# Decoder layer on one core: transposes in halves of 64 rows with new engine orders, cross attention's output weights folded into k^T v, and the local output projection as three products

## The reference

```python
def attn(x):     # 16 heads of 64, causal; rows are keys, columns queries of the score matrix as written
    q, k, v = einsum('ahe,bce->bach', W, x)          # for W_Q, W_K, W_V
    p = softmax(where(tril, einsum('bach,baCh->bacC', k, q), -1e10) / 8)
    return einsum('aeh,bach->bce', W_O, einsum('bacC,baCh->bach', p, v))

def xattn(x, ctx):  # linear attention, 16 heads of 16
    q, k = 1 + elu(x @ Wq.T + bq), 1 + elu(ctx @ Wk.T + bk);  v = ctx @ Wv.T + bv
    k = where(mask, 0, k);  q = l2norm over tokens(q);  k = l2norm over head features(k)
    kv = einsum('bhnd,bhne->bhde', k, v)
    return einsum('bhnd,bhde->bhne', q, kv) @ Wo.T + bo

def layer(x):    # twice: local attention, windows of 128, 8 heads of 64, then an MLP
    q, k, v = split(shift_token(x) @ wqkv)
    q, k = rotary_xpos(l2norm(q) * qs, l2norm(k) * ks)
    x = x + softmax(8 * q k^T over own and previous window) v @ wo
    a, g = split(layernorm(shift_token(x)) @ w1 + b1)
    return x + (a * gelu(g)) @ w2 + b2

x = x + attn(layernorm(x));  x = x + xattn(layernorm(x), ctx);  x = x + (layer(layer(z)) of z = layernorm(x))
```

## Time and profile before

| | us |
|---|---|
| median of 3 runs | 1154.78 |
| lowest, highest | 1153.16, 1154.82 |
| profiled execution | 1154.38 |
| its span, first to last instruction | 1152.6 |

### The profile page before, as it was taken

The page is one execution under the profiler, slowest core; times in us unless marked ns, Lnnn a source line. Parts: engine busy times, 40 slices in busy tenths (PEclk is TensorE's granted clock), DMA queues, the critical chain, the costliest instruction groups (busy, mean ns, idle before and its releaser), DMA issues.

```text
span 1152.6 us, 20639 instructions
## 1 busy us (share of the span) xinstructions
PE 1124.3 (98%) x7114; PEld 874.4 (76%) x7114; DVE 790.9 (69%) x2417; ACT 691.6 (60%) x1712; POOL 610.0 (53%) x641
## 2 busy tenths in 40 slices
PE   8999999999999999999999999999999999999997
PEld 6777777777777766767667887877878878787676
DVE  6867677667767356778897677768667686675553
ACT  3668677777767224453676647657656566575832
POOL 1456666666664322049896446557465474573330
PEclk9999999999999999999999999999999999999999
DMA  7003333323210401030040001200002100001010
GB/s 255 1 2 132 100 109 113 123 93 123 89 71 2 164 19 55 1 112 22 19 176 1 2 1 36 94 1 1 1 19 99 55 1 1 1 32 42 19 38 18
DMA packets 30310, 64.72 MB, mean 56 GB/s; under 512 B 3840, under 2 KB 16256, under 8 KB 29696
## 3 DMA queue, kind: packets, MB, share of 16 engines
q1 hardware_dynamic: 30208, 63.41, 15.7%
HBM read 41.04 MB, written 22.36 MB: 55 GB/s over the span
## 4 chain that ended last, share of the span: by engine, by line
PE 90%; DVE 4%; POOL 2%; ACT 2%; issue 1%; DMA 0%; DVEq 0%; ACTq 0%; POOLq 0%
PE psum L1532 48%; PE psum L1633 7%; PE psum L1598 6%; PE psum L1615 6%; PE psum L1765 5%; PE psum L1814 5%; PE psum L1799 4%; PE psum L1781 4%; PE psum L1747 2%; PE psum L1827 1%; PE psum L1838 1%; PE psum L1721 1%; POOL rn L780 1%; PE psum L1829 0%; DVE y L1091 0%
## 5 line engine op out<-in xcount | busy, mean ns | idle before, releaser
L735 POOL TENSOR_TENSOR probs<-probs,rden 128x128 f32<-128x128 f32 (+3 forms) x256 | 177.6, 725 | 80.6 <-DVE rden L1149 80.6
L974 ACT ACTIVATE lp<-lp,lneg,rn 128x256 f32<-128x256 f32 (+1 forms) x256 | 143.6, 568 | 11.6 <-DVE lneg L1366 11.5
L890 ACT ACTIVATE probs<-probs,negmax 128x128 f32<-128x128 f32 (+3 forms) x256 | 139.9, 553 | 5.8 <-DVE negmax L1144 5.8
L1134 DVE CUSTOM_DVE_ANT_0 probs<-psum,causal 128x128 f32<-128x128 f32 (+3 forms) x256 | 110.3, 487 | 19.4 <-PE psum L1598 19.3
L768 POOL TENSOR_TENSOR lp<-lp,lrden 128x128 f32<-128x128 f32 x64 | 25.6, 400 | 165.8 <-DVE lrden L1371 165.8
L780 POOL TENSOR_TENSOR rn<-ssm,neg_half 128x8 f32<-128x8 f32 x64 | 108.4, 1693 | 0.0
L1354 DVE CUSTOM_DVE_ANT_0 lp<-psum,local 128x256 f32<-128x256 f32 (+1 forms) x256 | 84.2, 385 | 20.6 <-PE psum L1765 20.6
L771 POOL TENSOR_TENSOR lp<-lp,lrden 128x768 f32<-128x768 f32 x64 | 93.9, 1467 | 0.0
L1532 PE MATMUL psum<-wqkv_hi,hT_lo 128*128 128x512 f32 x192 | 82.0, 427 | 0.1
L961 ACT ACTIVATE sq<-psum 128x512 f32<-128x512 f32 x64 | 38.0, 594 | 68.9 <-PE psum L1532 68.9
L1633 PE MATMUL psum<-pT,v 128*64 128x256 f32 (+3 forms) x512 | 77.7, 446 | 1.4 <-DVE pT L1158 1.0
(11 more groups left out here) (172 smaller groups left out, 3146.7 us busy)
## 6 DMA issues: line engine op xcount, KB each, us to landing
w_raw<-in_w_all SPq DMA_DIRECT2D x22, 380.0 KB, 3.1
w_scratch<-w_half SPq DMA_DIRECT2D x22, 380.0 KB, 2.3
w_scratch<-w_rest SPq DMA_DIRECT2D x22, 380.0 KB, 3.0
x<-in_x SPq DMA_DIRECT2D x8, 512.0 KB, 7.4
aw<-in_w_quads SPq DMA_DIRECT2D x4, 768.0 KB, 5.5
wqkv_lo<-w_scratch SPq DMA_DIRECT2D x6, 512.0 KB, 6.3
wqkv_hi<-w_scratch SPq DMA_DIRECT2D x6, 512.0 KB, 4.5
w_hi<-w_scratch SPq DMA_DIRECT2D x2, 1364.0 KB, 6.5
```

The source lines that it names most:

```text
L735: ins = pool.tensor_tensor(pr, pr, rden[:, u % 2, h, i:i + 1].broadcast_to([P, TRI[i]]), ALU.mult)
L890: ins = act.activation(pr, pr, ACT.Exp, bias=negmax[:, u % 2, h, i:i + 1], scale=ADH ** -0.5, accum_out=den[:, u % 2, h, i:i + 1])
L974: ins = act.activation(pr, pr, ACT.Exp, bias=lneg[:, u % 2, h, w:w + 1], scale=rn[:, m % 2, w, 0, 2 * j + h:2 * j + h + 1], accum_out=lden ...
L1134: ins = dve.tensor_tensor_reduce(probs[:, u % 2, h, TRI_AT[i]:TRI_AT[i + 1]], bank[:, at:at + TRI[i]], causal[:, S - TRI[i]:S], 1.0, -3e38 ...
```

## The change

1. Every transpose of probabilities (self and local attention) and of q and k (`Tqk`) is done as two: the upper and the lower 64 rows of the block apart, each against the 64 x 64 corner of the identity, into two different banks. The evictions take a bank of halves each and write them with a stride. Self attention's six groups become three (`t0`, `t1`, `t2`) of two banks each; `s` and `t` use other banks, `z` takes a bank in turn; VectorE's `sA` of unit u waits for the last transposes of unit u-2. `lqT` and `lkT` become one tile `lqkT`.
2. Cross attention: `xo` multiplies the masked k^T v (transposed) by `xwo` first, VectorE scales that (256 columns, out of PSUM) to `kvs`, and `xw` is the product of the queries with it. `oxT` and its copies are gone.
3. The local projection: `loT_hi` (ScalarE) and `loT_lo` (VectorE, a new item AV), weights `wo_hi` and `wo_lo` from the rounded weights in memory, three fp32r matmuls for one fp32 matmul.
4. All four engines' orders are written anew. A tile `room` that nothing uses, and a smaller scratch area for DMA.

```diff
-S_PARTS = {"sA": (0, 1), "sB": (2,)}
-S_BANKS = ((0, 1), (2, 3), (0, 1))
-T_BANKS = (4, 5, 2, 3, 4, 5)
+S_PARTS = {"sA": (0,), "sB": (1, 2)}
+S_BANKS = ((0, 1), (2, 3), (4, 5))
+T_BANKS = ((4, 5), (2, 3), (4, 5))
+T_BLOCKS = (((0, 0), (0, 1), (0, 3)), ((1, 0), (1, 1), (1, 3)), ((0, 2), (1, 2)))
...
-        UNIT_PE = ("sA@2 z sB@2 pv@2 pk@3 pq@3 t0@1 t1@1 t2@1 t3@1 t4@1 t5@1")
-        UNIT_DVE = ("sA@2 r0@1 z sB@2 r1@1 aw2@2 pk@3 aw0@3 t0@1 pq@3 aw1@3 t2@1 t4@1")
-        UNIT_ACT = ("e0@1 e1@1 pv@2 aw2@2 pk@3 aw0@3 pq@3 aw1@3 t1@1 t3@1 part@1 t5@1")
-        UNIT_POOL = ("f0@1 f1@1 part@1")
+        UNIT_PE = ("t0 t1 sA@2 t2 sB@2 z pk@3 pq@3 pv@3")
+        UNIT_DVE = ("pk aw0 pq t0@-2 t2@-2 r0@-1 aw1 t4@-2 sA sB z@-2 r1@-1 aw2")
+        UNIT_ACT = ("t1@-3 t3@-3 t5@-3 pv@-1 aw2@-1 e1@-2 part@-3 pk aw0 pq e0@-1 aw1")
+        UNIT_POOL = ("f1@-1 part@-2 f0")
...
-        STEP_PE = ("q2@1 hnT@-1 v2@1 k2@1 Ta1 Sa3 hid0@-1 Tb1 hid1@-1 Tqk1@1 Sb3 hid2@-1 q3@1 hid3@-1 k3@1 "
-                   "Tqk2@1 hid4@-1 hid5@-1 AV1 Ta2 v3@1 hT@2 w20@-1 Tqk3@1 q0@2 Tb2 Sa0@1 AV2 Sb0@1 k0@2 "
-                   "Ta3 q1@2 w21@-1 Tb3 k1@2 Sa1@1 AV3 Sb1@1 Ta0@1 wo0 wo1 v0@2 sh Tb0@1 v1@2 Sa2@1 AV0@1 "
-                   "Sb2@1 Tqk0@2")
+        STEP_PE = ("q2@1 hnT@-1 k2@1 v2@1 Ta1 Sa3 Tb1 hid0@-1 hid1@-1 Sb3 Tqk1@1 hid2@-1 q3@1 hid3@-1 k3@1 "
+                   "hid4@-1 hid5@-1 Tqk2@1 AV1 Ta2 v3@1 hT@2 w20@-1 q0@2 Tqk3@1 k0@2 Tb2 Sa0@1 AV2 Sb0@1 "
+                   "Ta3 q1@2 k1@2 Sa1@1 Tb3 w21@-1 AV3 Sb1@1 Ta0@1 v0@2 wo0 wo1 Sa2@1 Tb0@1 sh AV0@1 Sb2@1 "
+                   "Tqk0@2 v1@2")
+        STEP_DVE = ("Tqk3 Tb2@-1 fb3@-1 Sa0 q0@1 Ta3@-1 Sb0 k0@1 AV2@-1 fa0 Tb3@-1 Sa1 q1@1 w21@-2 AV3@-1 "
+                    "k1@1 Sb1 Ta0 fb0 wo0@-1 wo1@-1 stats@-1 fa1 Tb0 Sa2 norm@-1 AV0 apply@-1 fb1 Tqk0@1 Sb2 "
+                    "hnT@-1 Ta1 q2@1 k2@1 Tb1 Sa3 hid0@-1 hid1@-1 fa2 Sb3 Tqk1@1 hid2@-1 q3@1 hid3@-1 hs0@-1 "
+                    "k3@1 hs1@-1 fb2 hid4@-1 hs2@-1 Tqk2@1 hid5@-1 hs3@-1 hs4@-1 hs5@-1 Ta2 fa3 hT@2 AV1 "
+                    "w20@-1")
...
+                if u >= 2 and part == "sA":
+                    for n in (4, 5):
+                        wait_full(dve, plan["t", u - 2, n])
...
-                for e in range(E2):
-                    dve.tensor_scalar(kvs[:, s % 2, e, :], kvm[:, s, e, :], qss[:, s % 2, e:e + 1], None, ALU.mult)\
-                        .then_inc(kvs_done, 1)
+                use = plan["xo", s]
+                bank = wait_full(dve, use)
+                for e in range(E2):
+                    ins = dve.tensor_scalar(kvs[:, s % 2, e, :], bank[:, e * D:(e + 1) * D], qss[:, s % 2, e:e + 1],
+                                            None, ALU.mult)
+                ins.then_inc(read[use[0]], 1)
...
+            def rest_of_O(u):
+                use = plan["O", u]
+                bank = wait_full(dve, use)
+                dve.wait_ge(o_hi, u + 1)
+                j = FPAIRS - 1 - u % FPAIRS
+                dve.tensor_tensor(loT_lo[:, j, :], bank[:, :], loT_hi[:, j, :], ALU.subtract).then_inc(read[use[0]], 1)
...
+            def transposes(u, g):
+
+                pe.wait_ge(s_prob, 2 * u + (1 if g == 0 else 2))
+                uses = [plan["t", u, 2 * g + half] for half in range(2)]
+                banks_of = [wait_free(pe, use) for use in uses]
+                blocks = [(h, i, c) for h, c in T_BLOCKS[g] for i in range(c, T)]
+                for n, (h, i, c) in enumerate(blocks):
+                    lo = TRI_AT[i] + c * P
+                    for half in range(2):
+                        rows = slice(half * HP, (half + 1) * HP)
+                        ins = pe.transpose(banks_of[half][:, n * HP:(n + 1) * HP], probs[rows, u % 2, h, lo:lo + P],
+                                           ident[rows, rows])
+                        if n == len(blocks) - 1:
+                            ins.then_inc(full[uses[half][0]], 1)
...
-                    product(bank[:, :], [(kvs[:, b % 2, e, :], qT[:, b % 2, e, :])]).then_inc(full[use[0]], 1)
+                    ins = mm(bank[:, e * D:(e + 1) * D], kvm[:, b, e, :], xwo[:, e, :], start=True, stop=True)
...
-                                      [(oxT[:, b % 2, e, t * P:(t + 1) * P], xwo[:, e, :]) for e in range(E2)])
+                                      [(qT[:, b % 2, e, t * P:(t + 1) * P], kvs[:, b % 2, e, :]) for e in range(E2)])
...
-                        ins = mm(bank[:, i * D:(i + 1) * D], loT[:, FPAIRS - 1 - k, t * P:(t + 1) * P], wo[:, k, :],
-                                 start=i == 0 and k == 0, stop=i == 1 and k == FPAIRS - 1, skip_group_check=True)
+                        for term, (o, w) in enumerate(((loT_lo, wo_hi), (loT_hi, wo_lo), (loT_hi, wo_hi))):
+                            ins = mm(bank[:, i * D:(i + 1) * D], o[:, FPAIRS - 1 - k, rows], w[:, k, :],
+                                     start=i == 0 and k == 0 and term == 0,
+                                     stop=i == 1 and k == FPAIRS - 1 and term == 2, skip_group_check=True)
```

More of the change, by code:

```diff
@@ L484, in build @@
             if what == "t":
-                take((what, *at), T_BANKS[at[1]])
+                for half in range(2):
+                    take((what, at[0], 2 * at[1] + half), T_BANKS[at[1]][half])
             if what == "z":
-                take((what, *at), Z_BANK)
+                turn((what, *at), "p")
             if what == "awo":
@@ L894, in evac_pT @@
             def evac_pT(u, n):
-                h, k = divmod(n, 3)
                 use = plan["t", u, n]
-                bank = wait_full(act, use)
-                at = KEYB_AT[T_TILES[k][0]]
-                w = sum(KEYB[j] for j in T_TILES[k])
-                copy(pT[:, h, at:at + w], bank[:, 0:w]).then_inc(read[use[0]], 1)
+                src, dst = transposed(wait_full(act, use), n)
+                copy(dst, src).then_inc(read[use[0]], 1)
             def evac_x1T(b):
@@ L981, in evac_T @@
                 bank = wait_full(act, use)
-                copy(lpT[:, h, 0:S], bank[:, :]).then_inc(read[use[0]], 1)
+                copy(lpT[:, h, :].rearrange("p (b s q) -> p b s q", s=2, q=HP)[:, :, 0, :],
+                     bank[:, 0:LOC_N // 2].rearrange("p (b q) -> p b q", q=HP)).then_inc(read[use[0]], 1)
             def evac_O(u):
@@ L986, in evac_O @@
                 bank = wait_full(act, use)
-                copy(loT[:, FPAIRS - 1 - u % FPAIRS, :], bank[:, :]).then_inc(read[use[0]], 1)
+                copy(loT_hi[:, FPAIRS - 1 - u % FPAIRS, :], bank[:, :]).then_inc(o_hi, 1)
             def evac_hnT(m):
@@ L1506, in _ @@
                     evac_T(*at)
+                if what == "AV":
+                    rest_of_O(*at)
                 if what == "wo":
@@ L1741, in transposed_qk @@
             def transposed_qk(m, t):
-                for i, (what, done) in enumerate((("Tq", l_q), ("Tk", l_k))):
+                uses = [plan[what, m, t] for what in ("Tq", "Tk")]
+                banks_of = [wait_free(pe, use) for use in uses]
+                for i, done in enumerate((l_q, l_k)):
                     pe.wait_ge(done, T * m + t + 1)
-                    use = plan[what, m, t]
-                    bank = wait_free(pe, use)
                     for j in range(FPAIRS):
-                        ins = pe.transpose(bank[:, j * P:(j + 1) * P], ra[:, t % 2, i, j * P:(j + 1) * P], ident[:, :])
-                    ins.then_inc(full[use[0]], 1)
+                        at = (i * FPAIRS + j) * HP
+                        for half in range(2):
+                            rows = slice(half * HP, (half + 1) * HP)
+                            ins = pe.transpose(banks_of[half][:, at:at + HP], ra[rows, t % 2, i, j * P:(j + 1) * P],
+                                               ident[rows, rows])
+                            if i and j == FPAIRS - 1:
+                                ins.then_inc(full[uses[half][0]], 1)
             def local_scores(u, part):
```

174 lines of the change are left out of this document (84 added, 90 removed), and 69 rows, old and new, of tables (CLOSE_DVE, ENTRY_ACT, ENTRY_DVE, ENTRY_PE).

## The result

The changed kernel takes 1117.49 us (median of 4 runs, 1116.66 to 1118.54) against 1153.97 us before (4 runs beside it, 1151.73 to 1154.82): ratio 0.9687, 95% interval 0.9669 to 0.9706. The forecast was 1113 with a range of 1090 to 1145, so it is the first case of the four, pairs that overlap and a part of the gain turned into waits. The profiled execution spans 1114.6 us, 38.0 less than before; I had summed 41.5.

The account below looks back on a forecast made before the run. TensorE, busy 98% of the span, was taken as the bound. Terms -15.5 (self attention), -3.0 (cross attention), -1.5, -19.5 (local attention) and -2 sum to -41.5, from 1154.4 to 1113 us, range 1090 to 1145.

Parts of the forecast that it names:

- first case of the four: Whole kernel: half transposes overlap and part of the gain turns into waits; 1113 us, own range 1100 to 1130, chance 63%.
- start: Stretch before self attention's steady units: no change was forecast, 0 us.
- self attention: Self attention from 43 to 404 us: 29 intervals each 0.53 us shorter, -15.5 us.
- last units and cross attention: Cross attention: shorter xo passes give -3.4 us, three more changes of shape +0.4; -3.0 us in the sum.
- entry: Stretch from 520 to 604 us, bound by VectorE, which only gains work: -1.5 us, bounds 0 and -6.
- local steps: Local attention: each step 3.3 us shorter after waits, over 5.9 intervals, -19.5 us.
- last stage: Last 99 us, where TensorE already waits long: -2 us, bounds +1 and -6.
- price of a pair: TensorE's time for two half transposes: 0.060 us, bounds 0.054 and 0.22, against 0.109 for a whole one.
- Cases 3: Rival on half transposes: a pair's weight loads take turns, 0.109 us a pair; 1143 us, chance 19%.
- 4 (0.12 and more): Rival on half transposes: a pair costs more than a whole one; 1155 to 1159 us, or 1290 fully in turn; 8%.
- unit of self attention: One self attention unit: 11.24 us falls to 10.70, work alone to 9.99, with 0.71 of waits for ScalarE's copies.
- the one on lpT for Tb1: Local step: TensorE waits about 0.6 us before Tb1 while its banks are emptied.

Follow-up runs that it names:

- Experiment 1: The changed kernel with pk's product alone in PSUM bank 0, so that pv no longer takes its bank: 1115.69 us.
- experiment 2: The changed kernel with the exponentials e0 ahead of the copy kh in ScalarE's order of a unit: 1131.34 us.
- experiment 3: The changed kernel with both pk in bank 0 and e0 ahead of kh in ScalarE's order: 1106.59 us.
- experiment 6: The changed kernel with the local output projection back to one float32 product for three and no loT_lo: 1128.62 us.
- experiment 4: The changed kernel, new orders kept, with whole 128-row transposes back in self attention and the local stage: 1168.12 us.
- experiment 7: Three runs: cross attention's folding alone in the kernel before, 1156.76 us; folding undone in the changed kernel, 1130.50; changed kernel with each xo issued twice, 1121.34.
- Experiment 8: The changed kernel with GpSimd's last.6 moved ahead of norm.7 and sum.1 behind last.7, as before the change: 1114.73 us.
- Experiment 5: The kernel before with half transposes in the local stage alone, its own orders kept: 1148.01 us.

## Why the prediction was right, step by step

| stage, us | forecast | measured |
|---|---|---|
| start | 0 | -3.8 |
| self attention | -15.5 | -12.2 |
| last units and cross attention | -3.0 | -4.6 |
| entry | -1.5 | -1.2 |
| local steps | -19.5 | -18.2 |
| last stage | -2.0 | +1.9 |
| sum | -41.5 | -38.0 |

The measured column is distances between starts: the first z (43.13 and 40.33), the z of unit 28 (359.3 and 345.9), hT (502.16 and 481.71), the first projection (604.41 and 582.73), the seventh (1053.63 and 1013.78) and the end. The orders place sB and pv differently around z, so one sB (0.95) and one pv (1.5) are counted to the stage that they belong to. These are two single executions, and the clock did not fall at the same places in both; three of the rows hold 1.5 to 1.9 us of that, as said below.

**The price of a pair.** Taken at 0.060, measured 0.0625; the two loads of a pair run at once and the halves overlap. Cases 3 (0.11) and 4 (0.12 and more) are out. The Trainium skill ("TensorE: Matmul & The Clock Gate", "Step-by-step: what each phase is for") gives 62 ns for every MATMUL in one mode of decoding, by which a pair would take 0.124 us, an estimate. Two MATMULs in 0.0625 us show that this does not hold for these.

**The unit of self attention.** 10.71 forecast, 10.83 measured, and that near by luck: two mistakes nearly cancel. The waits were mis-placed: I had 0.71 us for ScalarE's copies before t2 and sB, in the trace it is 0.34 of pv for kl, on a bank that I had not followed through the order in which banks are handed out. That wait hid the one that I had. Experiment 1 shows mine once the other is gone (by the table 0.32 before t2 and 0.17 before sB, where I had 0.30 and 0.41), experiment 2 shows the other grown, experiment 3 neither. And TensorE's own time was too low, 10.00 for 10.40: sB was 1.24 for 1.60, because its first load stands exposed behind the transposes (217.80 to 218.08, 0.28 for 0.18, in the trace of experiment 3), and the step from one tile of scores to the next costs more too (0.24 and 0.20 where 0.18 and 0.12 are usual). I had priced the changes of shape around pv and z, not this one. The remaining 0.09 is for the most part pv's own first load, exposed behind its wait (1.58 for 1.50). The term was 29 x 0.53 = 15.5; measured are 27 intervals from z to z at 0.39 and 1.6 in the first, 12.2.

**The local step.** -3.3 forecast, -3.29 measured. By part: three products -1.24 (forecast -1.2, experiment 6), halves -2.52 under the new orders (experiment 4), which leaves +0.47 for the new orders with whole transposes. Halves and orders together are -2.05, for a forecast of -4.3 with 1.1 taken back by shapes and 1.1 by waits. The sum is right, the split was not: the listed waits are 0.3 a step and the one on lpT for Tb1 did not come. At the measured 0.0625 the pairs save 4.1, so changes of shape and pauses too short to be listed take back about 1.7, where I had 1.1 for shapes; no run tells the two apart.

**Cross attention.** The products fell by the forecast 3.4 us, of which about half arrives (experiment 7). t.29 to t.31 in halves, 60 blocks, bring up to 2.8, which my 29 intervals covered only in part. And part of the -4.6 is the clock of one execution. The traces of experiments 6 and 8 have the same code here and the same waits, yet from z of unit 28 to hT they take 137.3 and 137.4 us where the change took 135.8. The windows, of the change and of experiment 6 (columns as in the earlier trace rows):

```profile
366.00:386.00 20.00, 18.28 (x129) 13.66 (x129) 9.31 (x26) 3.64 (x8) 7.74 (x11) 1.00 0.08 28
366.00:386.00 20.00, 18.27 (x121) 13.70 (x121) 8.87 (x24) 4.04 (x10) 8.02 (x12) 0.91 0.08 30
```

The kernel before has such a fall as well (0.91 from 380 to 400 us). With one on either side this stage is -3.1, the forecast -3.0.

**The entry.** -1.5 forecast, -1.2 measured, with the fall to 0.79 from 570 to 575 us in it, which the kernel before does not have in this stage. In the trace with xo twice, without that fall, the entry is 99.6 us, 2.7 less than before.

**The start.** I had taken nothing. With whole transposes under the new orders z.0 starts at 42.01, with halves at 40.33: 1.7 us come with the halves, 0.9 of it the 20 blocks ahead of z.0, which I had left out. The other 2.1 (43.13 and the sB of 0.95 that before stood behind it, less 42.01) looks like the gain of the start's new order, and is nearly all clock. Experiment 5 has the start of the kernel before, with the same waits of TensorE in it (1.1 us, then 2.0 for kl), and its z.0 starts at 41.23. The kernel before, then experiment 5:

```profile
30.00:35.00 5.00, 5.00 (x36) 3.99 (x35) 2.84 (x12) 3.86 (x11) 2.85 (x5) 0.71 0.00 0
30.00:35.00 5.00, 5.00 (x40) 3.97 (x39) 4.13 (x21) 3.76 (x12) 4.55 (x8) 1.00 0.00 0
```

So 1.9 of the 3.8 us are a fall of the clock behind those waits, which the one execution had and the other had not; 0.2 are left for the order.

**The last stage.** This step failed: -2, bounds +1 and -6, measured +1.9. I had looked only at waits for data. The cause is GpSimd's two sums, moved in its order, which reach VectorE through no semaphore at all. Experiment 8 moves them back: 2.8 us by the medians, and the stage is then 97.1 us in its trace, 1.8 less than before, the forecast -2.

## What to carry to other kernels

A float32 transpose of 128 by 128 can be cut into two halves in different row groups and banks, at 0.0625 us for both in place of 0.109. Each change of the array's shape costs 0.15 to 0.20 us here, so the halves pay most where they stand beside other work of the same shape. A wait that shows in the trace may stand in front of another of nearly the same length: here one fix alone gave -2 us, the other +14, and both gave -11. So follow each engine's order past the first wait before judging a fix. When a resource changes users (z in the banks of pk, pq and pv), walk the whole sequence in which it is handed out. And before a difference of 1 or 2 us between the same stage of two traces is put down to the code, compare the granted clock of the stretch, and look for a third trace with the same code there.
